# Perceiver block on one core: self-attention scores of two head pairs in one row, and the last context chunk of a cross tile turned inside the output projection

## The reference, cut to what matters

```python
# cross attention: 64 contexts of 257 keys, width 384
q, k, v = hidden_states @ Wq, encoder_hidden_states @ Wk, encoder_hidden_states @ Wv
probs = softmax(einsum('bhsd,bhkd->bhsk', q, k) / sqrt(64))
out = einsum('bhsk,bhkd->bhsd', probs, v)  ->  out @ Wo + bo
# self attention: 32 tokens attend to the 32 of their own batch
scores = einsum('bhqd,bhkd->bhqk', q, k) + position_bias
ctx = softmax(scores) @ v  ->  ctx @ Wo
# feed-forward, weights and activations rounded to 8-bit steps
h = fake_quant(silu(xq @ w_gate.T) * (xq @ w_up.T));  y = h @ fake_quant(w_down).T
```

## Time and profile before

| | |
|---|---|
| runs | 1580.36, 1582.78, 1581.98 us; median 1581.98 |
| profiled execution | span 1580.3 us; the lowest time shown is 1580.36 |
| PE | busy 1543.1 us, 98% of the span |
| DVE, ACT, POOL | 67%, 47%, 23% |
| stages, us from the start | projections to 187, cross tiles to about 1017, self attention to about 1436, feed-forward to the end |

### The profile page before, as it was taken

How to read it: one execution, slowest core, us unless ns; L and a number is a source line. 1 busy time by engine, 2 the same in 40 slices (tenths; PEclk the granted TensorE clock), 3 DMA queues, 4 the chain that set the end, 5 groups by cost and what they waited for, 6 DMA issues and landing times.

```text
span 1580.3 us, 36115 instructions
## 1 busy us (share of the span) xinstructions
PE 1543.1 (98%) x13802; PEld 1287.0 (81%) x13802; DVE 1066.2 (67%) x2306; ACT 737.1 (47%) x1596; POOL 371.2 (23%) x225
## 2 busy tenths in 40 slices
PE   7999899999999999999999999999999999998989
PEld 6888788988999899888988898878878878786544
DVE  8766677677666766776667766657555664556788
ACT  5444656455545554555545554433123222224755
POOL 1000235343444344343434344400000000000000
PEclk9999999999999999999999999999999999999999
DMA  6898864341334223431434133250311311223022
GB/s 241 318 369 345 328 238 139 125 154 57 125 138 138 90 92 138 138 133 58 141 127 153 54 128 124 81 200 22 107 63 35 115 49 42 99 84 134 1 107 107
DMA packets 78958, 210.74 MB, mean 133 GB/s; under 512 B 5712, under 2 KB 31760, under 8 KB 76048
## 3 DMA queue, kind: packets, MB, share of 16 engines
q1 hardware_dynamic: 78864, 209.39, 36.9%
HBM read 140.42 MB, written 68.94 MB: 132 GB/s over the span
## 4 chain that ended last, share of the span: by engine, by line
PE 75%; issue 12%; DVE 8%; ACT 4%; DMA 0%; DVEq 0%; SPq 0%; ACTq 0%; POOLq 0%; POOL 0%
PE psum_o L694 13%; PE psum_s L671 7%; PE psum_q L671 7%; PE psum_o L1488 6%; PE psum_q L1528 6%; PE psum_q L1488 6%; PE psum_t L1560 6%; PE psum_o L559 5%; PE psum_o L709 5%; DVE qk L1092 3%; PE psum_t L682 3%; PE psum_t L640 2%; PE psum_s L1515 1%; PE psum_t L591 1%; PE psum_q L591 1%
## 5 line engine op out<-in xcount | busy, mean ns | idle before, releaser
L694 PE MATMUL psum_o<-pT,c_nat 128*128 128x512 f32 x1152 | 307.3, 403 | 3.4 <-issue 2.4
L694 PEld LDWEIGHTS psum_o<-pT,c_nat 128*128 128x128 f32 x1152 | 202.7, 189 | 38.7 <-DVE pT L957 3.6
L1304 POOL TENSOR_TENSOR c_nat<-c_raw,constants 128x768 fp32r<-128x768 f32 x64 | 93.8, 1466 | 560.1 <-PE psum_o L694 445.3
L1158 DVE TENSOR_SCALAR oT<-psum_o,c_last 128x512 f32<-128x512 f32 x192 | 143.7, 748 | 65.5 <-PE psum_o L694 65.5
L671 PE MATMUL psum_s<-cT,qk 128*128 128x256 f32 (+1 forms) x1152 | 167.7, 288 | 2.3 <-DVE cT L957 0.3
L671 PEld LDWEIGHTS psum_s<-cT,qk 128*128 128x128 f32 x1152 | 151.0, 189 | 11.3 <-DVE cT L957 5.2
L671 PE MATMUL psum_q<-cT,qk 128*128 128x256 f32 (+1 forms) x1152 | 152.8, 284 | 1.0 <-DVE qk L1092 1.0
L884 ACT ACTIVATE probs<-psum_s,nmax 128x257 f32<-128x257 f32 x128 | 61.1, 477 | 197.7 <-DVE nmax L1173 197.7
L671 PEld LDWEIGHTS psum_q<-cT,qk 128*128 128x128 f32 x1152 | 143.3, 190 | 4.0 <-issue 2.6
L957 DVE TENSOR_TENSOR pT<-psum_t,pT 128x512 fp32r<-128x512 f32 x128 | 87.8, 687 | 70.9 <-ACT pT L775 70.9
L1289 POOL TENSOR_TENSOR c_raw<-c_raw,last_row 128x768 f32<-128x768 f32 x64 | 120.3, 1881 | 29.5 <-DMA last_row<-in_ctx_dram 19.1
(11 more groups left out here) (295 smaller groups left out, 3118.2 us busy)
## 6 DMA issues: line engine op xcount, KB each, us to landing
qk_by_tile<-staged SPq DMA_DIRECT2D x32, 1536.0 KB, 10.1
raw<-qk_by_tile SPq DMA_DIRECT2D x16, 3072.0 KB, 12.3
c_raw<-in_ctx_dram SPq DMA_DIRECT2D x64, 384.0 KB, 3.3
last_row<-in_ctx_dram SPq DMA_DIRECT2D x64, 192.0 KB, 4.0
out_dram<-x_out SPq DMA_DIRECT2D x32, 256.0 KB, 2.0
x_res<-in_x_dram SPq DMA_DIRECT2D x16, 256.0 KB, 2.7
x_in<-out_dram SPq DMA_DIRECT2D x4, 1024.0 KB, 8.5
x_all<-out_dram SPq DMA_DIRECT2D x1, 4096.0 KB, 13.3
```

The source lines that it names most:

```text
L694: i = pe.matmul(ps[:], c_nat[(b - 1) % 2][:, part, k, m * P:(m + 1) * P], pT[:, moving, k, :], start=(k, part, moving) == (0, 0, 0), stop= ...
L1158: nc.vector.tensor_scalar(oT[:, m, :, (b - 1) % 4, :], ps[:].rearrange("p (s q) -> p s q", q=SQ), c_last[:, (b - 1) % 2, m:m + 1], None, A ...
```

## The change

Three things. In the self attention `pe_self_scores` takes two head pairs at a time (argument `two`): four rows of the loop instead of eight, each of 64 matmuls, into the same two banks (256 columns instead of 128 of each); the query buffers become three; DVE adds the bias with one instruction of 256 columns per bank. The third query buffer takes half of the gap behind `pT2`, so the last down chunk moves to the end of the key weight's high part, its rounding moves behind the last key product in ACT's order, and the chunk before it is now the one in two pieces. In the cross tiles of sections "second" and "loop", chunk 2 of step 3 is turned after 12 of the 24 matmuls of the output projection, and DVE's subtraction of that chunk moves between pieces 2 and 3 of the next queries.

```diff
@@ self_units, and pe_self_all in the same way
-            if j:
-                u += [(("SC", s, j - 1, par), ("s0", "s1")[par]) for par in range(2)]
+            if j in (2, 4, 6):
+                u += [(("SC", s, j // 2 - 1, par), ("s0", "s1")[par]) for par in range(2)]
...
-        u += [(("SC", s, 7, par), ("s0", "s1")[par]) for par in range(2)]
+        u += [(("SC", s, 3, par), ("s0", "s1")[par]) for par in range(2)]
@@ pe_wo
             for k in range(KI):
+                if k == KI // 2 and section in ("second", "loop"):
+                    pe_ctxT(pe, t, 3, section, (2,))
@@ pe_cross_tile
-                if before and (more or b < 3):
+                if before and (more or b < 3) and not (b == 3 and begun):
                     pe_ctxT(pe, t, b, section, (2,))
@@ dve_cross_tile
                 if qk_next:
                     dve_qk_low(dve, t + 1, 2, section)
+                    ctxT(b, 2)
                     dve_qk_low(dve, t + 1, 3, section)
...
-                if after:
+                if after and not qk_next:
                     ctxT(b, 2)
@@ pe_self_scores
+            pairs = (2 * two, 2 * two + 1)
+            for j in pairs:
+                taken(pe, own(("Q", s, j)))
+                taken(pe, own(("K", s, j)))
+            places = [empty(pe, own(("SC", s, two, par))) for par in range(2)]
+            for a, j in enumerate(pairs):
+                for i in range(GROUP):
+                    at = slice((GROUP * a + i) * SQ, (GROUP * a + i + 1) * SQ)
...
+                            m = pe.matmul(places[par][0][rows_, at], q2[j % 3][r, i, rows_], k2[j % 2][r, i, rows_],
+                                          start=True, stop=True)
@@ act_round_weights
+            if n == KD - 1:
+                full(act, own(("K", GROUPS - 1, 7)))
@@ act_self_all
-                    if j < 7 and chunk_at(s, j + 1) is not None:
+                    if j < 7 and chunk_at(s, j + 1) is not None and (s, j) != (GROUPS - 1, 6):
                         act_round_weights(act, chunk_at(s, j + 1))
+                    if (s, j) == (GROUPS - 1, 7):
+                        act_round_weights(act, chunk_at(s, j))
@@ dve_self_scores
+                heads = slice(4 * two + par, 4 * two + par + 3, 2)
+                nc.vector.tensor_tensor(pr2[:, :, heads, :].rearrange("p t a k -> p a t k"),
+                                        ps[:, 0:2 * GROUP * SQ].rearrange("p (a t k) -> p a t k", t=GROUP, k=SQ),
+                                        bias[:, heads, :].rearrange("p a (t k) -> p a t k", t=1).to_broadcast([P, 2, GROUP, SQ]),
+                                        ALU.add).then_inc(free, 1)
@@ sp_self_all
-                        sp.wait_ge(s_wround, c + 1)
+                        sp.wait_ge(s_wround, c + 2 if c == FC + 2 else c + 1)
```

More of the change, by code:

```diff
@@ L324, in build_kernel @@
         pT2 = [sb(f"pT2_{i}", [P, HEADS, SQ], F32) for i in range(2)]
-        sb.at += 2 * HEADS * SQ * 4
+        q2.append(sb("q2_2", [P, GROUP, P], F32))
+        BETWEEN = sb.at
+        sb.at += HEADS * SQ * 4
         v2 = [sb(f"v2_{i}", [P, INNER], F32) for i in range(2)]
@@ L349, in build_kernel @@
         assert aT2_last.shape[2] == KI and GROUP * D * 4 == 2 * KI * P * 4
-        IN2, BETWEEN = SELF_AT["x_in2"], SELF_AT["pT2_1"] + HEADS * SQ * 4
-        wd_whole = [nc.alloc_sbuf_tensor_at(f"wd_whole{n}", [P, HID], BF16, offset=at)
-                    for n, at in enumerate((IN2, IN2 + 2 * HID, BETWEEN))]
+        IN2, LATE = SELF_AT["x_in2"], SELF_AT["w2k_high"] + GROUP * INNER * 4 - 3072
+        wd_whole = {n: nc.alloc_sbuf_tensor_at(f"wd_whole{n}", [P, HID], BF16, offset=at)
+                    for n, at in ((0, IN2), (1, IN2 + 2 * HID), (3, LATE))}
         WD_CUT = (FC - 1) * P
         wd_front = nc.alloc_sbuf_tensor_at("wd_front", [P, WD_CUT], BF16, offset=IN2 + 4 * HID)
-        wd_back = nc.alloc_sbuf_tensor_at("wd_back", [P, P], BF16, offset=BETWEEN + 2 * HID)
-        assert 4 * HID + 2 * WD_CUT <= GROUP * D * 4 and 2 * HID + 2 * P <= 2 * HEADS * SQ * 4
+        wd_back = nc.alloc_sbuf_tensor_at("wd_back", [P, P], BF16, offset=BETWEEN)
+        assert 4 * HID + 2 * WD_CUT <= GROUP * D * 4 and 2 * P <= HEADS * SQ * 4
         chosen = nc.alloc_sbuf_tensor_at("chosen", [P, SQ // KPB, P], F32, offset=CT1_AT)
@@ L367, in build_kernel @@
         x_res_last = nc.alloc_sbuf_tensor_at("x_res_last", [P, 2, D], F32, offset=sb.at)
+        assert sb.at + 2 * D * 4 <= LATE
         h_all = sb("h_all", [P, NCH, FC, 512], F32)
@@ L1503, in pe_self_k, with pe_self_scores @@
             pe_wide(pe, ("K", s, j), "k", j)
[L1505 to L1518, removed]
+        def pe_self_scores(pe, s, two):
+            pairs = (2 * two, 2 * two + 1)
[6 more added lines that the diff above has]
+                    at = slice((GROUP * a + i) * SQ, (GROUP * a + i + 1) * SQ)
+                    for par in range(2):
+                        r = slice(64 * par, 64 * par + 64)
+                        for b in range(4):
+                            rows_ = slice(SQ * b, SQ * b + SQ)
+                            m = pe.matmul(places[par][0][rows_, at], q2[j % 3][r, i, rows_], k2[j % 2][r, i, rows_],
+                                          start=True, stop=True)
+                        if (a, i) == (1, GROUP - 1):
+                            m.then_inc(places[par][1], 1)
         def pe_self_v(pe, s, i, n):
@@ L1574, in wd_block @@
         def wd_block(n, k):
-            if n < KD - 1:
+            if n in wd_whole:
                 return wd_whole[n][:, k * P:(k + 1) * P]
@@ L1614, in pe_self_all @@
                         pe_self_q(pe, s, j)
-                        pe_self_scores(pe, s, j - 1)
+                    if j in (2, 4, 6):
+                        pe_self_scores(pe, s, j // 2 - 1)
                     pe_self_k(pe, s, j)
@@ L1619, in pe_self_all @@
                 pe_self_v(pe, s, 0, 0)
-                pe_self_scores(pe, s, 7)
+                pe_self_scores(pe, s, 3)
                 pe_self_v(pe, s, 0, 1)
@@ L1652, in act_self_q @@
         def act_self_q(act, s, j):
-            act_copy(act, own(("Q", s, j)), flat(q2[j % 2][:]))
+            act_copy(act, own(("Q", s, j)), flat(q2[j % 3][:]))
         def act_self_k(act, s, j):
@@ L1744, in dve_self_x, with dve_self_scores @@
                         lambda ps: ps[:].rearrange("p (k n) -> p k n", k=KD))
-        def dve_self_scores(dve, s, j):
-            if (s, j) == (0, 0):
+        def dve_self_scores(dve, s, two):
+            if (s, two) == (0, 0):
                 taken(dve, own(("BIAS",)))
             for par in range(2):
[L1751 to L1754, removed]
+                heads = slice(4 * two + par, 4 * two + par + 3, 2)
+                ps, free = full(dve, own(("SC", s, two, par)))
+                nc.vector.tensor_tensor(pr2[:, :, heads, :].rearrange("p t a k -> p a t k"),
+                                        ps[:, 0:2 * GROUP * SQ].rearrange("p (a t k) -> p a t k", t=GROUP, k=SQ),
+                                        bias[:, heads, :].rearrange("p a (t k) -> p a t k", t=1).to_broadcast([P, 2, GROUP, SQ]),
+                                        ALU.add).then_inc(free, 1)
         def dve_self_max(dve, s, i, ch):
@@ L1760, in dve_self_max @@
                 for par in range(2):
-                    taken(dve, own(("SC", s, 7, par)))
+                    taken(dve, own(("SC", s, 3, par)))
             ch.link(V.tensor_reduce(mx2[:, i, :], pr2[:, i, :, :], AX_X, ALU.max))
@@ L1893, in dve_self_all @@
                 for j in range(8):
-                    if j:
-                        dve_self_scores(dve, s, j - 1)
+                    if j in (2, 4, 6):
+                        dve_self_scores(dve, s, j // 2 - 1)
                     if j == 0 and s:
@@ L1914, in dve_self_all @@
                     dve_turned(dve, chunk_at(s, 7))
-                dve_self_scores(dve, s, 7)
+                dve_self_scores(dve, s, 3)
                 dve_self_max(dve, s, 0, ch)
```

## The result

| | before | after |
|---|---|---|
| median, us | 1582.08 (1580.36 to 1582.78, 4 executions) | 1572.91 (1571.98 to 1574.02, 4 executions) |
| ratio to before | | 0.9941, 95% interval 0.9928 to 0.9954 |
| profiled span, us | 1580.3 | 1570.2 |

By the ratio the changed kernel is 9.3 us faster (between 7.3 and 11.4); the medians differ by 9.2. The forecast was 9.4 us, a median of 1572.6 and a span of about 1570.9.

A forecast was written before the change was run, and what follows sets the result against it. PE, busy for 98% of the span, was taken as the bound, so only its idle or dearer time could be won. Cross tiles 4.6 plus merged score rows 4.8 made 9.4 us: 1582.0 to 1572.6, range 1568.4 to 1577.4.

The forecast's parts named there:

- Part 1: Cross tile ends: PE's wait ahead of the third context chunk's scores goes at 14 tile ends, saving 4.6 us.
- Part 2: Self-attention scores, two pairs a row: 64 added passes at 9.7 ns cost 0.62 of 0.92 us; 16 mergers save 4.8 us.
- Both bounds: Self-attention score mergers: at least 3.2 us saved by the attended block's cost, at most 9.0 at the first passes' pace.
- quick start: Score row: the first 32 passes begin within 0.18 us, 5.6 ns each; a merged row gets one such start instead of two.
- the queue of 64: TensorE's instruction queue: 32 passes with their loads fill it during the gap; saving 4.8 us by this rule, 9.0 without.
- the floor of 25 ns: TensorE matmuls start no less than about 25 ns apart, however short; by that the result would be 6.3 us slower, 1588.3.
- What was costed at nothing: Rest of the self-attention merger: waits, buffers, DVE's wider additions, with 1.1 us in hand ahead of the attended block.
- Part 3: Down chunks: last chunk's load waits for two roundings, its rounding moves in ACT's queue; nothing, bound 1 us either way.
- (a): Cross tiles: the chunk's gain turns into another wait, mid-projection or at the product behind; 1577.2 us, chance 0.07.
- (b): Self-attention scores: the merged row saves nothing, its gap growing or passes slowing to 14.4 ns; 1577.4 us, chance 0.07.
- (c): Cross tiles and scores: both (a) and (b), so the change does nothing; 1582.0 us, chance 0.06.
- (d): Merged row's passes 33 to 128 come one after another, 29 ns each; 1592.1 us, loss above 18.9 ns, chance 0.04.

The follow-up runs named there:

- PE's alone: The changed kernel with DVE's subtraction of the context chunk back at its old place, PE still turning it inside the projection: 1576.45 us, ratio 0.9966 to before.
- DVE's alone: The changed kernel with PE turning the context chunk behind the projection again, DVE still subtracting it ahead of query piece 3: 1581.05 us, ratio 0.9994 to before.
- parts 2 and 3 alone: The changed kernel with its cross-tile edits undone, so cross tiles as before: 1576.73 us, ratio 0.9963 to before.
- the runs of one part each: The kernel before with only the cross-tile edits: 1577.56 us, ratio 0.9966; the changed kernel with those edits undone: 1576.73 us, ratio 0.9963.
- the same doubling in the other kernel: The kernel before with every self-attention score matmul issued twice, 32 rows of 128 passes: 1609.38 us, ratio 1.0169 to before.
- the run with 256 passes a row: The changed kernel with every self-attention score matmul issued twice, the second over the first: 1658.42 us, ratio 1.0484 to before.

## Why the prediction was right

The mechanism was right in both parts. That the forecast of 9.4 us met the medians' 9.2 so closely is partly luck: the interval is 4 us wide, and two errors in part 2 go in opposite directions.

**Part 1** was forecast at 4.6 us and gave 4.5 by the tile distance and 4.7 by the span of its run (5.3 by its median). The step from the timeline to the cause (DVE's order, not PE's) is shown by the two halves: with PE's alone the gap stays, with DVE's alone a dearer one comes.

**Part 2** was forecast at 4.8 us and gave 5.4 net by the span of its run (6.1 by its median). Two of its terms were a little off, in opposite directions. A late pass costs 8.3 ns, not 9.7; with it the added 64 passes cost 1.47 - 0.92 = 0.55 us instead of 0.62, and a merger saves 0.37 instead of 0.30, 5.9 us for 16. The other term was missing: gaps that look like a want of instructions, one of 0.5 us in the profile after and one of 0.9 in that of parts 2 and 3 alone. Both bounds held, 3.2 and 9.0 us. The merged row has one quick start of 32 passes. Of the two rules that the prediction took from the Trainium skill, "TensorE: Matmul & The Clock Gate", the trace after agrees with the queue of 64 (32 passes and their loads in the quick start) and not with the floor of 25 ns (8.3 ns from pass to pass).

**What was costed at nothing.** DVE's two additions of 256 columns take 0.76 us, forecast about 0.8. The end of the softmax and the start of the attended block of group 0 (DVE, PEld):

```profile
1074.70 0.76 DVE L1768 TENSOR_TENSOR pr<-psum_s,bias 128x256 f32<-128x256 f32 x2 [0.53 <-PE psum_s L1525]
```

```profile
1081.06 0.71 DVE L1795 STREAM_TRANSPOSE pT<-pr 128x512 f32<-128x512 f32 x1
```

```profile
1083.51 0.13 PEld L1552 LDWEIGHTS psum_s<-pT,v 32*64 32x64 f32 x2 [0.35 <-issue]
```

1081.06 + 0.71 = 1081.77 against 1083.51 - 0.35 = 1083.16 leaves 1.4 us in hand, where 1.1 was forecast, and line 1552 has no gap other than its 16 of before. Part 3 brings no new entry in the waits of PEld; it was not run by itself.

**The rivals.** (a) and (b) fall by the runs of one part each, (c) with both. (d) needed 18.9 ns for a late pass; 8.3 is less than half of it.

## What to carry to other kernels

Where the bounding engine waits for a helper, move the producer's and the consumer's instruction together and check both margins: half of part 1 was worth nothing, the other half lost more than there was to win. Small matmuls that fill a gap between wide ones are paid for by the visit, and each visit less saved 0.37 us here, so fewer and longer visits win, up to a length at which PE stops in mid-row, it seems for want of instructions: 16 rows of 128 passes had one or two such gaps of 0.2 to 0.9 us an execution, 16 rows of 256 one of 0.4 to 4.3 us in every row. A doubled operation prices it only if the doubling brings no new limit; the same doubling in the other kernel showed here that it did.

## What the runs showed of the hardware that was not expected

**PE can stop in mid-row, it seems for want of instructions.** In the run with 256 passes a row, PE stopped after 176 and after 246 passes, with nothing to wait for. The queue named "instruction", whole execution, in the kernel after and in this run (packets, MB, share):

```profile
q8 instruction: 71, 1.16, 0.3%
```

```profile
q8 instruction: 87, 1.43, 0.4%
```

The only difference between the two programs is 2,048 passes with their loads, 4,096 instructions of PE, and these make 16 packets more, so this queue carries PE's instructions. The DMA queues of that kernel in the first gap, first 1036.0 to 1039.5, which has no packet of instructions, then 1039.5 to 1040.6 (packets, MB, share of 16 engines):

```profile
q1 hardware_dynamic: 681, 1.42, 104.0%
```

```profile
q1 hardware_dynamic: 214, 0.42, 99.7%
q8 instruction: 1, 0.02, 5.0%
```

Data loads fill the DMA engines throughout; the packet lands at 1040.54 and PE goes on at 1042.04. In all 16 second gaps PE goes on 1.2 to 1.6 us after such a packet has landed. The 0.50 us gap at line 1538 of the kernel after is alike: a packet lands at 1074.16 and PE's loads go on at 1075.45. The Trainium skill, "Runtime: NRT & Kernel Launch", section "Terms", has an instruction memory per engine that is refilled in blocks of 16 KiB; the packets have that size (0.02 MB). That PE waits for just these packets is inferred from the count and the order of events. Full DMA engines are not needed for such a gap, as one of 2.11 us, in which next to nothing else is moved, shows (windows as above):

```profile
1182.90:1184.90 2.00, 0.06 (x2) 0.00 (x0) 0.00 (x0) 0.00 (x0) 0.00 (x0) 1.00 0.00 0
```

Whether the loads made the gap of 4.31 us the longest was not tried.

**A score matmul issued again,** on the same piece of the array and over the same result, cost 10.9 ns a pass by the distance of rows; added matmuls on other pieces cost 0.55 us / 64 = 8.6 ns by the same measure.

**The clock after a stop.** Behind the gap of 4.31 us the granted clock was 0.50 in the window of 4 us shown above, 1.2 GHz. In the window of the 2.11 us gap it was 1.00. In the kernel after, with gaps of 0.5 us at most in the self attention, no such fall is seen there.
